# A layer of attention and a gated network on one core: maximum scores and exponent products before gate and up in every slot

## The chip, the core and the metric

One NeuronCore of a Trainium2 chip runs the whole program. The metric is the device time of one execution in microseconds. Five engines take part, each with its own queue that it works off in order: PE (matrix products), ACT (activations, and a DMA queue), DVE (vector), POOL (element-wise work on SBUF), SP (DMA issues). They are held together by semaphores alone.

## What is computed

Sixteen sequences of 256 tokens and width 256 go through one layer with the norm behind each part:

```python
qkv = x @ Wqkv + bqkv                     # 16 query heads of 16, 4 key/value groups
scores = einsum('bqhd,bkhd->bhqk', q, k) / HD
out = softmax(scores) @ v ; x = layernorm(x + out @ Wout + bout)
gate, up = split(x @ ternary(w_gate_up).T)   # 1024 each
h = silu(gate) * up
x = layernorm(x + rms_norm(h) @ ternary(w_proj).T)
```

## The kernel before

The program is a pipeline of slots, eight to a sequence (SLOTS = 8, line 37), 172 in all. Every engine has a function `slot(n)` that lists what it does in slot n, in a fixed order; `run_slots` (line 176) plays slots 0 to 63 written out, 64 to 127 as a loop over 16 slots, and the rest written out. A step starts at an offset (lines 39 to 87) behind the first slot of its sequence: `n.once(X)` is true in one slot of eight, `n.chunk(X)` in eight in a row, one chunk in each. So a slot holds work of up to six sequences at a time. In the middle, a slot with t modulo 8 = m always holds the same work.

What PE does in a slot, in its order (lines 570 to 647):

- gate and up of one chunk of 128 hidden rows (`gate_up`, line 507, chunk offset 31): eight products into ffn_ps. They wait for x1T_lo (the low part of the transposed first norm, once a sequence, slot 7) and for h_done of the chunk before, since ffn_ps has room for one chunk.
- the first maximum group (`max_scores(n, st, 0)`, offset 9): two products into one of three short banks, from which DVE takes the row maxima (line 776).
- the exponent products (`exp_scores`, offset 15): two products of 512 columns into exp_ps, which ACT turns into probs (line 690).
- the steps that come once a sequence: transposes of x (slot 1), v (slot 7), the shift rows (slots 5 and, late, 1), projections of q and k (slot 2), of the output (slot 3), transposes of x1 (slot 5), of pv (slots 6 and 0).
- the second maximum group, probs times v (odd slots), and down (`down`, line 521, offset 33) of a chunk that was gated two slots earlier.

The three short banks are handed out by BANK_TABLE (lines 94 to 101): for each slot modulo 8, which bank each user takes. `use_short` (line 478) makes PE wait until the last user of the same bank has been read. Of it:

```python
BANK_TABLE = {0: {"max0": 1, "pv1": 0, "max1": 2},
...
              2: {"max0": 0, "q": 2, "max1": 0, "k": 1, "att": 2},
              3: {"max0": 0, "max1": 1, "o": 2},
              4: {"max0": 1, "max1": 0},
              5: {"max0": 2, "shift0": 0, "max1": 1, "x1": 2},
              6: {"max0": 0, "pv0": 1, "max1": 0},
              7: {"max0": 2, "v": 0, "max1": 1, "sq": 2}}
```

The user "x1" of slot 5 is released by x1T_lo (line 467), the maximum groups by max_taken.

ACT, in its order (lines 677 to 754): tanh of gate (line 681), the copy of xT (slot 1), the exponent (line 690), q, the copy of pv (slots 3 and 7), the high part of h and its square, the high part of x1T (slot 5), k, the transposed attention, the copy of y (slot 0), and at the end of slots 5 and 1 two DMA issues that put the shift rows of the softmax into q_st (line 746); they wait for DVE's shift_split.

DVE, in its order (lines 811 to 905): the first maximum, gated (line 817), h_f (line 824, releases ffn_ps), the low part of x1T (X1_LOW, slot 6, line 828), the first shift split (slot 5), the residual and statistics of the second norm (LN2_STATS, slot 2, lines 836 to 844), the second maximum, then the division of pv (slots 6, 0), v, the apply step of the first norm (slot 4, line 880), the second shift split (slot 1), the apply step of the second norm (slot 4, line 890), the residual and statistics of the first norm (slot 3, lines 895 to 902), the low part of k.

POOL makes the low part of h and the sum of squares, and SP issues the transfers. SP's stacking of queries and keys for the maximum groups waits for exp_scored (lines 411 and 418).

Of the kernel before, what the change touches and what calls it, by code (L numbers as in the profile page):

```python
# [18 lines left out]
ACT = mybir.ActivationFunctionType  # L19
# [29 lines left out]
EXP0 = 15  # L49
# [9 lines left out]
FFN0 = 31  # L59
# [107 lines left out]
def wait(eng, sem, value):  # L167

    if isinstance(value, int):
        if value > 0:  # L170
            eng.wait_ge(sem, value)
    else:
        eng.wait_ge(sem, value)
# [26 lines left out]
def postln_layer(nc, x, Wqkv, bqkv, Wout, bout, w_gate_up, w_proj, out):  # L200
    ctx = ExitStack()
    with ctx:
        def sb(name, shape, dt=F32):
            return ctx.enter_context(nc.sbuf_tensor(name, shape, dt))

        def ps(name, shape, dt=F32):
            return ctx.enter_context(nc.psum_tensor(name, shape, dt))

        def sem(name):
            return ctx.enter_context(nc.semaphore(name))  # L210
# [46 lines left out]
        probs = sb("probs", [P, 4, TT, 2, S])  # L257
# [29 lines left out]
        exp_ps = ps("exp_ps", [P, TT, 2 * S])  # L287
# [31 lines left out]
        exp_scored, exp_done = sem("exp_scored"), sem("exp_done")  # L319
        pv_done, pv_copied, pv_turned = sem("pv_done"), sem("pv_copied"), sem("pv_turned")  # L320
# [29 lines left out]
        def alternate(n, st):  # L350

            return n.it is None and n.t >= TWO_BANKS and st.s % 2 == 1

        def gate_up_bank(n, st, half):
            return exp_ps[:, half, 0:S] if alternate(n, st) else ffn_ps[:, half, :]
# [86 lines left out]
        def _(pe):  # L442
            def products(dst, lhs, rhs, start=True, stop=True):

                pairs = list(zip(lhs, rhs))
                for i, (a, b) in enumerate(pairs):
                    last = pe.matmul(dst, a, b, start=start and i == 0, stop=stop and i == len(pairs) - 1)  # L447
                return last
# [29 lines left out]
            def use_short(n, name):  # L478

                if found := previous_use(n, SHORT_ORDER.index(name), short_users[BANK[n.t % SLOTS, name]]):  # L480
                    st, (_, _, released, per, extra) = found
                    wait(pe, released, st.count(per, extra))
                return short(n, name)
# [14 lines left out]
            def exp_scores(st):  # L498

                wait(pe, shift_loaded[st.s // 4], st.count(32, 32))  # L500
                wait(pe, exp_done, st.count(8, st.s))
                for t in range(TT):
                    last = pe.matmul(exp_ps[:, t, :], k_st[:, st.par, st.s % 4, t * P:(t + 1) * P],  # L503
                                     q_st[:, st.par, first_head(st.s):first_head(st.s) + 5:4, :], start=True, stop=True)
                last.then_inc(exp_scored, 1)

            def gate_up(n, st):
                wait(pe, x1T_lo, st.count(1, 1))
                if st.it is None and st.b == 0 and st.s == 0:
                    pe.wait_ge(w_ev, len(pieces))  # L510
                if alternate(n, st) and n.t - SLOTS < TWO_BANKS and st.s == 1:
                    wait(pe, exp_done, SLOTS * B)
                wait(pe, h_done, st.count(8, st.s - 1 if n.it is None and n.t > TWO_BANKS else st.s))
                for half in range(2):
                    c = half * F + st.s * P
                    last = products(gate_up_bank(n, st, half),
                                    [wguT[:, k, c:c + P] for k in range(DT) for _ in range(2)],
                                    [x1T[a][:, st.par, k, :] for k in range(DT) for a in range(2)])
                last.then_inc(ffn_made, 1)
# [29 lines left out]
            def turn(bank, src, done):  # L549

                for i, blk in enumerate(src):
                    last = pe.transpose(bank[:, i * P:(i + 1) * P], blk, ident[:])  # L552
                last.then_inc(done, 1)
# [6 lines left out]
            def keep_clock(n, count):  # L560

                if n.it is not None or not CLOCK_FROM <= n.t < CLOCK_TO:
                    return
                turned = sum(at + W_TURN < n.t for at in W_READ)
                if turned:
                    pe.wait_ge(w_ev, turned - 1)
                for _ in range(count):
                    pe.matmul(turn_banks[turned % 2][:, 0, 0:P], ident[:], ident[:], start=True, stop=True)

            def slot(n):  # L570
                if st := n.chunk(FFN0):
                    gate_up(n, st)
                if st := n.chunk(MAX0):
                    if st.it is None and st.b == 0 and st.s == 0:
                        pe.wait_ge(k_ones, 1)
# [3 lines left out]
                if st := n.chunk(EXP0):  # L579
                    exp_scores(st)  # L580
                keep_clock(n, 2)
                if st := n.once(X_T):
                    bank = use_short(n, "x")
                    wait(pe, x_loaded[st.par], st.count2(16, 16))
                    turn(bank, [xn[:, st.par, t, k * P:(k + 1) * P] for k in range(DT) for t in range(TT)], xT_made)
# [55 lines left out]
                if st := n.once(SUM_SQ):  # L641
# [5 lines left out]
                    last.then_inc(sq_summed, 1)  # L647

            run_slots(pe, slot)


        @block.scalar
        def _(act):
# [17 lines left out]
            def high(dst, src):  # L671
                return act.activation(dst, src, ACT.Identity)  # L672

            def both(n, name):
                return short(n, name)[:].rearrange("p (k t) -> p k t", k=2)

            def slot(n):
                if st := n.chunk(FFN0):
                    wait(act, ffn_made, st.count(8, st.s + 1))
                    wait(act, gated_done, st.count(8, st.s - 1))  # L680
                    act.activation(tanh[:, st.s % 2, :], gate_up_bank(n, st, 0), ACT.Tanh, scale=0.5  # L681
                                   ).then_inc(tanh_done, 1)
                if st := n.once(X_HIGH):
                    wait(act, xT_made, st.count(1, 1))
                    wait(act, k_made, st.count(1, 0))
                    high(xT[:], both(n, "x")).then_inc(xT_copied, 1)
                if st := n.chunk(EXP0):
                    wait(act, exp_scored, st.count(8, st.s + 1))
                    wait(act, pv_done, st.count(4, st.s // 2 - 1))
                    act.activation(probs[:, st.s % 4], exp_ps[:], ACT.Exp).then_inc(exp_done, 1)  # L690
                if st := n.once(Q_COPY):
                    if st.it is None and st.b == 0:
                        act.wait_ge(bias_loaded, 16 * 2)
# [59 lines left out]
                if (c := piece(n, 0)) is not None:  # L753
                    read_weights(c)

            run_slots(act, slot)


# [236 lines left out]
```

## Time and profile before

| | |
|---|---|
| median of 3 runs | 626.21 us (624.43 to 627.9) |
| the profiled execution | 624.11 us |
| its span | 622.1 us |
| mean granted TensorE clock | 0.975 |
| PE busy | 556.9 us, 90% |
| DVE busy | 457.7 us, 74% |
| ACT busy | 373.6 us, 60% |
| POOL busy | 288.7 us, 46% |

The span is from the first to the last instruction of the profiled execution; the time of an execution has some 2 us around it. Matmuls overlap in the pipeline, so a row's duration for one matmul is longer than the distance from its start to the next one's start; the distance is what it costs. The arrow behind a row of the timeline names whose end ended the idle time before it.

### The profile page before, as it was taken

What the parts mean: (1) busy time and instruction counts of PE and PEld (TensorE: products, weight loads), DVE (VectorE), ACT (ScalarE), POOL (GpSimd) and SP (SyncE); (2) the same over time, 40 slices, a digit from 0 to 9 for tenths busy, and PEclk for the clock granted to TensorE, in tenths of its full rate; (3) what the DMA queues carried; (4) which work ended last, traced back from release to release, by engine and by line L of the source; (5) the groups of instructions that cost most, each with busy time, mean ns of one, the idle gap of its engine ahead of it and who ended that gap; (6) DMA issues with size and microseconds to landing.
All of it is one profiled execution on the core that took longest, in us unless ns stands there. A gap on an engine that the chain in (4) does not pass through costs nothing.

```text
span 622.1 us, 14146 instructions
## 1 busy us (share of the span) xinstructions
PE 556.9 (90%) x4368; PEld 465.6 (75%) x4368; DVE 457.7 (74%) x1066; ACT 373.6 (60%) x738; POOL 288.7 (46%) x404
## 2 busy tenths in 40 slices
PE   5668989999999999999899999999999999899772
PEld 4656768788788787878787877778787877777762
DVE  7785875777877878787878787877878787755753
ACT  4454645666666666757566666666666756575442
POOL 5432331353536353535435453536354535455763
PEclk9697999999999999999999999999999999999996
DMA  7963354444352517061624344352617070101001
GB/s 232 153 131 44 79 86 95 71 95 69 78 104 69 113 45 138 23 136 25 146 35 115 65 98 80 77 102 61 118 43 136 17 144 5 36 3 35 18 0 35
DMA packets 53932, 49.08 MB, mean 79 GB/s; under 512 B 6144, under 2 KB 53888, under 8 KB 53888
## 3 DMA queue, kind: packets, MB, share of 16 engines
q1 hardware_dynamic: 51152, 47.60, 37.1%
q10 hardware_dynamic: 2736, 0.92, 0.6%
q8 instruction: 24, 0.39, 0.3%
q14 instruction: 20, 0.16, 0.1%
HBM read 33.29 MB, written 14.68 MB: 77 GB/s over the span
## 4 chain that ended last, share of the span: by engine, by line
PE 56%; DVE 25%; issue 9%; POOL 4%; ACT 3%; ACTq 2%; DMA 1%; DVEq 0%; POOLq 0%; SPq 0%
PE ffn_ps L447 13%; PE short_ps L447 10%; PE pv_ps L544 8%; PE short_ps L494 6%; PE exp_ps L503 5%; PE down_ps L529 5%; DVE row_max L776 5%; PE short_ps L552 4%; DVE w_hat L809 3%; DVE gated L817 3%; DVE x L880 2%; DVE st L898 2%; DVE h_f L824 2%; DVE r L895 2%; ACTq L746 2%
## 5 line engine op out<-in xcount | busy, mean ns | idle before, releaser
L776 DVE TENSOR_REDUCE row_max<-short_ps 128x2 f32<-128x512 f32 x256 | 173.7, 682 | 47.5 <-PE short_ps L494 47.4
L933 POOL TENSOR_TENSOR h_lo<-h_f,h_hi 128x256 fp32r<-128x256 f32 x128 | 94.8, 740 | 237.5 <-ACT h_hi L672 227.0
L690 ACT ACTIVATE probs<-exp_ps 128x1024 f32<-128x1024 f32 x128 | 130.9, 1023 | 32.7 <-PE exp_ps L503 30.7
L447 PE MATMUL ffn_ps<-x1T_hi,wguT 128*128 128x256 f32 x480 | 125.6, 295 | 21.0 <-DVE x1T_lo L765 10.7
L494 PE MATMUL short_ps<-k_st,q_st 65*128 65x256 f32 x512 | 116.4, 309 | 12.8 <-DVE row_max L776 12.4
L447 PE MATMUL ffn_ps<-x1T_lo,wguT 128*128 128x256 f32 x480 | 118.8, 281 | 0.0
L447 PEld LDWEIGHTS ffn_ps<-x1T_hi,wguT 128*128 128x128 f32 x480 | 90.4, 188 | 30.5 <-DVE h_f L824 13.9
L681 ACT ACTIVATE tanh<-ffn_ps 128x256 f32<-128x256 f32 x120 | 45.8, 381 | 104.3 <-PE ffn_ps L447 83.3
L494 PEld LDWEIGHTS short_ps<-k_st,q_st 65*128 65x128 f32 x512 | 82.1, 192 | 23.7 <-DVE row_max L776 12.3
L447 PEld LDWEIGHTS ffn_ps<-x1T_lo,wguT 128*128 128x128 f32 x480 | 90.5, 189 | 0.0
L938 POOL TENSOR_TENSOR sq_sum<-sq_sum,h_sq 128x256 f32<-128x256 f32 x112 | 82.9, 741 | 0.0
L503 PE MATMUL exp_ps<-q_st,k_st 67*128 67x512 f32 x256 | 81.2, 398 | 0.1
L529 PE MATMUL down_ps<-wpT,h_hi 128*128 128x256 f32 x256 | 75.7, 318 | 3.4 <-POOL h_lo L933 3.4
L672 ACT ACTIVATE h_hi<-h_f 128x256 fp32r<-128x256 f32 x128 | 52.9, 414 | 35.6 <-DVE h_f L824 33.3
L544 PE MATMUL pv_ps<-probs,v_ones 128*32 128x256 f32 x1024 | 69.4, 389 | 0.0
L529 PE MATMUL down_ps<-wpT,h_lo 128*128 128x256 f32 x256 | 66.4, 281 | 0.0
L817 DVE SCALAR_TENSOR_TENSOR gated<-tanh,ffn_ps 128x256 f32<-128x256 f32 x120 | 49.4, 411 | 17.8 <-ACT tanh L681 17.8
L529 PEld LDWEIGHTS down_ps<-wpT,h_hi 128*128 128x128 f32 x256 | 48.6, 190 | 16.4 <-issue 11.5
L824 DVE TENSOR_TENSOR h_f<-gated,ffn_ps 128x256 f32<-128x256 f32 x120 | 50.5, 421 | 5.4 <-DVE gated L817 1.6
L529 PEld LDWEIGHTS down_ps<-wpT,h_lo 128*128 128x128 f32 x256 | 48.7, 190 | 0.4
L447 PE MATMUL short_ps<-xT,wqkv 128*128 128x256 f32 x192 | 47.5, 384 | 0.0
L722 ACT ACTIVATE h_sq<-h_f 128x256 f32<-128x256 f32 x112 | 45.2, 404 | 0.0
(98 smaller groups left out, 864.6 us busy)
## 6 DMA issues: line engine op xcount, KB each, us to landing
q_st<-q_dram SPq DMA_DIRECT2D x128, 128.0 KB, 4.1
q_dram<-q_p SPq DMA_DIRECT2D x16, 512.0 KB, 3.0
xn<-in_L_attn_x_dram SPq DMA_DIRECT2D x16, 256.0 KB, 4.6
k_st<-k_dram SPq DMA_DIRECT2D x64, 64.0 KB, 2.3
res<-in_L_attn_x_dram SPq DMA_DIRECT2D x16, 256.0 KB, 3.3
out_dram<-y_out SPq DMA_DIRECT2D x16, 256.0 KB, 2.2
wgu_raw<-in_L_ffn_w_gate_up_dram SPq DMA_DIRECT2D x8, 256.0 KB, 6.5
k_dram<-k_p SPq DMA_DIRECT2D x16, 128.0 KB, 3.1
```

The costliest lines, as they stand in the source:

```text
L447: last = pe.matmul(dst, a, b, start=start and i == 0, stop=stop and i == len(pairs) - 1)
L494: last = pe.matmul(bank[:, t * S:(t + 1) * S], q_st[0:PAD, st.par, head, t * P:(t + 1) * P], k_st[0:PAD, st.par, st.s % 4, :], start=True, ...
L503: last = pe.matmul(exp_ps[:, t, :], k_st[:, st.par, st.s % 4, t * P:(t + 1) * P], q_st[:, st.par, first_head(st.s):first_head(st.s) + 5:4, ...
L529: last = pe.matmul(down_ps[:, t, :], h_p[a][:, st.s % 4, t * P:(t + 1) * P], wpT[:, st.s, :], start=(st.s == 0 and t == 0 and a == 0), sto ...
L544: last = pe.matmul(pv_ps[r:r + 32, s % 4 // 2, :], v_ones[:, st.par, t, s % 4, :], probs[:, s % 4, t, i, :], start=(t == 0), stop=(t == TT ...
L672: return act.activation(dst, src, ACT.Identity)
L690: act.activation(probs[:, st.s % 4], exp_ps[:], ACT.Exp).then_inc(exp_done, 1)
L776: dve.tensor_reduce(row_max[:, st.par, head * TT:(head + 1) * TT], short(n, f"max{i}")[:].rearrange("p (t k) -> p t k", t=TT), AX.X, ALU.m ...
L817: dve.scalar_tensor_tensor(gated[:, st.s % 2, :], tanh[:, st.s % 2, :], 1.0, gate_up_bank(n, st, 1), ALU.add, ALU.mult).then_inc(gated_don ...
L824: dve.tensor_tensor(h_f[:, st.s % 2, :], gated[:, st.s % 2, :], gate_up_bank(n, st, 0), ALU.mult).then_inc(h_done, 1)
L933: pool.tensor_tensor(h_p[1][:, st.s % 4, :], h_f[:, st.s % 2, :], h_p[0][:, st.s % 4, :].bitcast(F32), ALU.subtract).then_inc(h_lo, 1)
L938: pool.tensor_tensor(sq_sum[:, st.par, :], sq_sum[:, st.par, :], h_sq[:, st.s % 2, :], ALU.add).then_inc(h_summed, 1)
```

## The change

In PE's `slot`, the call of `gate_up` moves from the front of the slot to behind the first maximum group and the exponent products (and behind the clock-keeping products of `keep_clock`, which exist only in slots 2 to 29). In ACT's `slot`, the exponent moves in front of tanh, and so also in front of the copy of xT. DVE, POOL and SP keep their order; BANK_TABLE, SHORT_ORDER and every semaphore count stay as they are. The diff in full:

```diff
--- before.py
+++ after.py
@@ -568,8 +568,6 @@
                     pe.matmul(turn_banks[turned % 2][:, 0, 0:P], ident[:], ident[:], start=True, stop=True)
 
             def slot(n):
-                if st := n.chunk(FFN0):
-                    gate_up(n, st)
                 if st := n.chunk(MAX0):
                     if st.it is None and st.b == 0 and st.s == 0:
                         pe.wait_ge(k_ones, 1)
@@ -579,6 +577,8 @@
                 if st := n.chunk(EXP0):
                     exp_scores(st)
                 keep_clock(n, 2)
+                if st := n.chunk(FFN0):
+                    gate_up(n, st)
                 if st := n.once(X_T):
                     bank = use_short(n, "x")
                     wait(pe, x_loaded[st.par], st.count2(16, 16))
@@ -675,6 +675,10 @@
                 return short(n, name)[:].rearrange("p (k t) -> p k t", k=2)
 
             def slot(n):
+                if st := n.chunk(EXP0):
+                    wait(act, exp_scored, st.count(8, st.s + 1))
+                    wait(act, pv_done, st.count(4, st.s // 2 - 1))
+                    act.activation(probs[:, st.s % 4], exp_ps[:], ACT.Exp).then_inc(exp_done, 1)
                 if st := n.chunk(FFN0):
                     wait(act, ffn_made, st.count(8, st.s + 1))
                     wait(act, gated_done, st.count(8, st.s - 1))
@@ -684,10 +688,6 @@
                     wait(act, xT_made, st.count(1, 1))
                     wait(act, k_made, st.count(1, 0))
                     high(xT[:], both(n, "x")).then_inc(xT_copied, 1)
-                if st := n.chunk(EXP0):
-                    wait(act, exp_scored, st.count(8, st.s + 1))
-                    wait(act, pv_done, st.count(4, st.s // 2 - 1))
-                    act.activation(probs[:, st.s % 4], exp_ps[:], ACT.Exp).then_inc(exp_done, 1)
                 if st := n.once(Q_COPY):
                     if st.it is None and st.b == 0:
                         act.wait_ge(bias_loaded, 16 * 2)
```

## Rows read from the trace of the kernel before

**Rows 1.** The page's first part: busy us, share of the span, instructions.

```profile
PE 556.9 (90%) x4368; PEld 465.6 (75%) x4368; DVE 457.7 (74%) x1066; ACT 373.6 (60%) x738; POOL 288.7 (46%) x404
```

**Rows 2.** Windows: PE, PEld, DVE, ACT, POOL busy (instructions), PEclk, DMA share, GB/s.

```profile
342.59:375.82 33.23, 32.08 (x256) 26.77 (x257) 25.84 (x63) 21.58 (x44) 15.99 (x24) 1.00 0.41 84
560.00:590.00 30.00, 25.48 (x205) 22.38 (x204) 20.54 (x52) 14.89 (x37) 18.66 (x28) 1.00 0.07 18
```

**Rows 3.** Waits of PE, 75 to 575 us: total us, times, longest.

```profile
PE ffn_ps L447 <- DVE h_f L824: 9.0, 16, 1.0
PE ffn_ps L447 <- DVE x1T_lo L765: 8.4, 14, 1.3
PE short_ps L494 <- DVE row_max L776: 4.3, 4, 1.5
```

**Rows 4.** Timeline of PE, slots 3 to 5: start us, duration us, line, tiles.

```profile
337.99 0.66 PE L552 MATMUL short_ps<-ident,x 128*128 128x128 f32 x4
...
359.49 0.28 PE L447 MATMUL ffn_ps<-x1T_hi,wguT 128*128 128x256 f32 x1
...
360.44 0.40 PE L494 MATMUL short_ps<-k_st,q_st 65*128 65x256 f32 x2
360.68 0.63 PE L503 MATMUL exp_ps<-q_st,k_st 67*128 67x512 f32 x2
361.15 0.40 PE L494 MATMUL short_ps<-k_st,q_st 65*128 65x256 f32 x2
...
364.78 0.28 PE L447 MATMUL ffn_ps<-x1T_hi,wguT 128*128 128x256 f32 x1
...
367.81 0.39 PE L447 MATMUL ffn_ps<-x1T_hi,wguT 128*128 128x256 f32 x1 [0.50 <-DVE h_f L824]
```

**Rows 5.** Timelines of PE and of ACT, slot 4: exponent products, then the exponent.

```profile
365.97 0.62 PE L503 MATMUL exp_ps<-q_st,k_st 67*128 67x512 f32 x2
...
366.63 1.03 ACT L690 ACTIVATE probs<-exp_ps 128x1024 f32<-128x1024 f32 x1 [0.32 <-PE exp_ps L503]
```

**Rows 6.** Timeline of ACT, slot 6 (ACTq: its queue, issuing a DMA).

```profile
339.79 0.61 ACTq L746 DMA_DIRECT2D q_st<-shift_lo  x1
340.56 0.38 ACT L681 ACTIVATE tanh<-ffn_ps 128x256 f32<-128x256 f32 x1 [0.61 <-PE ffn_ps L447]
340.84 1.02 ACT L690 ACTIVATE probs<-exp_ps 128x1024 f32<-128x1024 f32 x1
341.89 0.42 ACT L672 ACTIVATE h_hi<-h_f 128x256 fp32r<-128x256 f32 x1
```

**Rows 7.** Timeline of PE: first rows of slot 6 and of slot 7.

```profile
338.97 0.28 PE L447 MATMUL ffn_ps<-x1T_hi,wguT 128*128 128x256 f32 x1
...
342.59 0.39 PE L447 MATMUL ffn_ps<-x1T_hi,wguT 128*128 128x256 f32 x1 [0.51 <-DVE x1T_lo L765]
```

**Rows 8.** Timeline of ACT, slot 2.

```profile
355.42 0.61 ACTq L746 DMA_DIRECT2D q_st<-shift_lo  x1
356.20 0.38 ACT L681 ACTIVATE tanh<-ffn_ps 128x256 f32<-128x256 f32 x1 [1.84 <-issue]
```

**Rows 9.** Timeline of DVE, slot 6.

```profile
340.98 0.42 DVE L817 SCALAR_TENSOR_TENSOR gated<-tanh,ffn_ps 128x256 f32<-128x256 f32 x1
...
341.77 0.68 DVE L765 TENSOR_TENSOR x1T_lo<-short_ps,x1T_hi 128x512 fp32r<-128x512 f32 x1
```

**Rows 10.** Timeline of DVE, slots 5, 2 (three rows) and 4.

```profile
337.26 0.67 DVE L776 TENSOR_REDUCE row_max<-short_ps 128x2 f32<-128x512 f32 x1
...
356.62 0.42 DVE L817 SCALAR_TENSOR_TENSOR gated<-tanh,ffn_ps 128x256 f32<-128x256 f32 x1 [0.48 <-ACT tanh L681]
...
357.41 0.87 DVE L836 SCALAR_TENSOR_TENSOR r<-y_sb,inv,x 128x256 f32<-128x256 f32 x2
...
359.27 0.67 DVE L776 TENSOR_REDUCE row_max<-short_ps 128x2 f32<-128x512 f32 x1
...
366.89 0.41 DVE L817 SCALAR_TENSOR_TENSOR gated<-tanh,ffn_ps 128x256 f32<-128x256 f32 x1
```

## The prediction

> **What bounds the kernel now.** The page's first part comes first: PE is busy for 90% of the span [rows 1]. Then the windows: one turn of the pipeline (eight slots, from slot 7 to the next slot 7) lasts 33.23 us and holds 32.08 us of PE work, at a granted clock of 1.00, which is 2.4 GHz [rows 2]. So in the middle PE is the bound and 1.15 us a turn is all that another order can win. Third, the waits of PE in that stretch: 16 times for h_f, 14 times for x1T_lo, four times for row_max [rows 3], so the first two are one a turn. The reader is to see in them where the 1.15 us lie: 0.50 us in front of gate and up of slot 5 (h_f) [rows 4], 0.51 us in front of those of slot 7 (x1T_lo) [rows 7], and 0.14 us in smaller pieces. PE hardly ever waits for a bank (row_max). Last, the timelines of the three engines: which instruction of ACT and DVE is late where, and how much room is left.
>
> I name slots by t modulo 8, and S is a slot's start on PE. A group of gate and up takes PE 0.95 us (359.49 to 360.44), a first maximum group M 0.24 us (to 360.68), the exponent products E 0.47 us (to 361.15) [rows 4]. Old order: gate/up at S, M at S+0.95, E at S+1.19. New order: M at S, E at S+0.24, gate/up at S+0.71. Either way the three end at S+1.66. No instruction, byte or wait is added; waits come earlier or later in their queues, and that is all that can cost.
>
> **Part A: the exponent in front of tanh, on ACT.** In a slot where ACT is free this costs nothing: exp_ps is ready 0.66 us after E starts (365.97 to 366.63 [rows 5]), so at S+0.90; an exponent holds ACT for 1.05 us (340.84 to 341.89 [rows 6]), so tanh can start at S+1.95, and gate/up, which started at S+0.71, are only ready at about S+1.9. But two slots of eight begin with ACT late. The two DMA issues of the shift rows (line 746) stand at the end of ACT's slots 5 and 1, behind a wait for DVE. The second issue ends at 340.40 in slot 6 (339.79 plus 0.61), the slot having begun at 338.97 [rows 6, 7], and tanh follows at 340.56, the exponent behind it [rows 6] (its row names PE as the releaser, but gate/up had been issued by 338.97 + 0.95 = 339.92; the issue came last). With the order turned round the exponent (ready at S+0.90 = 339.87) takes the place at 340.56 and tanh comes at 341.61: 1.05 us later. The same in slot 2: second issue until 356.03, tanh at 356.20 [rows 8], after the change at 357.25.
>
> *Slots 6 and 7.* gated follows tanh by 0.42 us, and x1T_lo starts 0.79 us after gated [rows 6, 9]. PE stands still for x1T_lo already: 0.51 us of idle, then gate/up of slot 7 at 342.59 [rows 7]. All of 1.05 us therefore reaches PE. One would hope that M and E, now in front, fill the gap. They can't: M of slot 7 uses bank 2 (BANK_TABLE), whose user before it is x1 of slot 5, and its release is x1T_lo itself. So the whole slot starts when gate/up would have: **+1.05 us a turn**, 13 times (t = 38 to 134; at t = 142 no shift DMA is left): **+13.7 us**. Bounds: 0 if ACT had room, and 1.05 plus the 0.71 us of M and E if these lay in series with anything, which the code doesn't show; I take the value of the rows.
>
> *Slots 2 and 3.* tanh, gated and h_f slip by 1.05 us. h_f itself isn't urgent in this long slot, but DVE does the statistics of the second norm next, and only then the maximum of the second group: gated at 356.62, r at 357.41, row_max at 359.27 [rows 10]. A wait of PE on a bank ends 0.73 us after such a row_max starts (337.26 [rows 10] to 337.99 [rows 4], the turn of x1). Today bank 0 is thus free at 360.00, 0.51 us after slot 3 begins at 359.49 [rows 4]; nobody notices, since M comes at 360.44, covered by gate/up. After the change M of slot 3 stands at the queue's head and wants this very bank 0 (second group of slot 2 and M of slot 3 share it). Its cover is gone: 0.51 us plus 1.05 us = **1.56 us of new idle a turn**, with E and gate/up queued behind M. It happens where the second norm runs in slot 2 and a maximum follows in slot 3, t = 42 to 130, 12 times: **+18.7 us**. Bounds: 0.51 us (the order on PE alone, 6 us in all) and 1.56 us plus the longest wait of this kind on record, 1.5 us [rows 3].
>
> **Part B: gate and up later, on PE.** Slot 5 gains: its gate/up need h_f of slot 4 and now have M and E in front. But what counts in slots 4 and 5 is DVE's queue, from the first norm's residual in slot 3 through both norms' apply steps to the maximum of M in slot 5; the turn of x1 waits for that maximum (bank 2 again: row_max at 337.26 [rows 10], PE at 337.99 [rows 4]). So the 0.50 us are only moved. Does this DVE chain get longer? In slot 4 gated starts at 366.89 [rows 10]. With S = 364.78 [rows 4], exp_ps is ready at 365.68, tanh starts at 366.73 and gated at 367.15: **0.26 us later**, 12 times: **+3.1 us**. Between 0 and 0.5 us a turn are possible.
>
> The 0.14 us of small idle (slots 0 and 1, gate/up waiting for h_f) go, since h_f has 0.71 us more: **-0.12 us** 13 times, **-1.6 us**.
>
> **Costed at nothing.** exp_scored comes 0.95 us earlier, and SP's stacking of queries and keys waits for it (lines 411 and 418): those transfers serve a slot some six later, DMA is busy 0.41 of the turn [rows 2], and without that cover a late one would cost its delay once a turn. Y_COPY now stands in front of an exponent in slot 1 and may push its tanh by 0.6 us; slot 1's second maximum then frees bank 0 some 0.3 us late for slot 2, but the wait of slot 2 for the shift DMA absorbs it. Slots before t = 31 have no gate/up, slots from 143 no exponent: nothing changes there.
>
> **Sum.** 13.7 + 18.7 + 3.1 - 1.6 = +33.9 us. The profiled execution took 624.1 us (span 622.1), so 658.0 us. It lies 2.1 us below the median of the runs shown, 626.21; for a median I add these: **660 us**. A turn should grow from 33.23 to about 35.9 us.
>
> **Rivals.**
> *R1, faster.* The mechanism is the cover of M and E in front of gate/up: if ACT has room in slots 2 and 6 (if the DMA issue doesn't hold the exponent as it holds tanh), h_f and x1T_lo are asked for 0.71 us later and all the idle of a turn, 1.15 us, goes: 13 x 1.15 = 15 us, 611 us. For it speaks that PE's two large waits [rows 3] both stand in front of gate/up. Against it: line 746 on ACT's own queue [rows 6, 8], and the banks. It decides at a delay of tanh under 0.2 us in slot 6 and a row_max of slot 2 over 0.5 us earlier than I have it. 5%.
> *R2, one wait of the two.* Slot 3 doesn't stall in full (DVE catches up): 660 - 18.7 = 641 us; or slot 7 doesn't: 646 us. For it speaks that a queue shifted as a whole may find new room; against it that both paths are without a gap in the rows. 14%.
> *R3, nothing.* The turned order leaves the same last waits and they end when they did, because the DVE chain of slots 3 to 5 sets the turn and the rest has slack: 626 us. Against it: PE's idle is 1.15 us a turn, so slack is scarce. 4%.
> *R4, the clock falls.* The granted clock of the turn shown is 1.00 [rows 2]; in the drain, with PE busy 25.48 of 30 us (15% idle), it is 1.00 too [rows 2], and after the change PE would be idle about 3.9 of 35.9 us, 11%. If it fell to 1.2 GHz nonetheless behind the two new waits, slot 3 (5.29 us, 359.49 to 364.78 [rows 4]) and slot 7 (taken as a mean slot, 33.23 / 8 = 4.15 us) would double: 12 x 9.4 = 113 us, 773 us. The Trainium skill, TensorE: Matmul & The Clock Gate, section A second HAM failure mode: psum-queue depth-cycling, speaks for it: a kernel that cycles through PSUM banks idles a little between its matmul groups so often that the clock swings between its two levels. By that rule this kernel should swing already; the rows at 1.00 don't show it. 3%.
>
> **How the numbers follow.** Forecast 74%, R1 5%, R2 14%, R3 4%, R4 3%. The forecast's own spread comes from its bounds: each of the two waits 0.3 us more or less a turn is 8 us, some late turn of DVE or a second issue of long duration a few more: 650 to 671. To leave no more than 2 in 10 out, the range takes in R2 nearly whole: **642 to 671**. About 0.5% (3 us) is what a measurement of this kernel can tell from no change. Faster by more: R1, 0.05. Within: R3, 0.04. Slower: 0.91.
>
> **What would show it.** Right: PE's waits list row_max in front of M (line 494) some 12 times with 1.5 us and x1T_lo now in front of M, not of gate/up, with about 1.6 us; in slot 6 the exponent directly behind the DMA issue and tanh 1.05 us later; h_f gone as a reason for PE's waits but for slot 5; clock 1.00; PE busy unchanged at 557 us, share down to 85%. Wrong: tanh of slots 2 and 6 no later than now, or M of slot 3 without idle before it; a row_max of slot 2 that waits for PE rather than for DVE's statistics; a turn under 34 us.

## The result and the profile after

The changed kernel takes 660.36 us (median of 4 runs, 657.91 to 663.27) against 625.32 us (median of 4, 623.56 to 627.9): 1.056 times as long, 95% interval 1.050 to 1.062. The forecast was 660 us, range 642 to 671. Ratios and intervals leave out the runs that are more than 1.5% above the fastest of their kernel (below: two of e2's four, one each of e4's, of e7's and of the last group's kernel before); medians are over all runs. The profiled execution has a span of 659.4 us at a mean granted clock of 0.964 (before: 622.1 us, 0.975).

First part of the page, then PE's waits between 141 and 545 us (total us, times, longest), of the changed kernel:

```profile
PE 568.9 (86%) x4368; PEld 472.7 (72%) x4368; DVE 460.5 (70%) x1066; ACT 365.7 (55%) x738; POOL 288.6 (44%) x404
...
PE short_ps L494 <- DVE x1T_lo L765: 12.9, 12, 1.1
PE short_ps L494 <- DVE row_max L776: 11.4, 15, 0.9
PE short_ps L552 <- DVE row_max L776: 9.1, 11, 0.9
```

[rows 3] named gate and up (L447) as what waited, for h_f and for x1T_lo. In this stretch nobody waits there any more. What waits are the two maximum groups at the head of slots 7 and 3 (L494) and the turn of x1 in slot 5 (L552), about once a turn each; row_max comes a few times more, for M of slot 2. The waits are shorter than forecast (1.5 us for row_max and 1.6 for x1T_lo): 0.9 and 1.1 us at most; where the rest went is worked out in the section on why the prediction was right.

Windows of the changed kernel: a turn in the middle, the first turn with gate and up, and two pieces of the last full one (PE, PEld, DVE, ACT, POOL busy, then PEclk, DMA share, GB/s).

```profile
359.79:395.30 35.51, 32.46 (x256) 26.88 (x256) 26.06 (x64) 21.00 (x43) 15.97 (x23) 1.00 0.37 78
...
110.91:146.36 35.45, 33.30 (x249) 27.19 (x247) 23.70 (x54) 20.79 (x41) 13.08 (x18) 0.95 0.42 79
...
547.00:556.00 9.00, 5.98 (x52) 4.61 (x50) 6.19 (x18) 4.95 (x11) 5.29 (x8) 1.00 0.02 5
556.00:565.00 9.00, 8.27 (x41) 6.19 (x42) 2.85 (x8) 2.62 (x5) 2.56 (x5) 0.62 0.00 1
```

The turn has gone from 33.23 us [rows 2] to 35.51 us, with 32.46 us of PE busy for 32.08 (the same matmuls, a few rows longer behind a wait): 1.9 us more of every turn are idle. The last two rows are something the prediction did not have: PE is busy for only 5.98 of 9 us, and in the 9 us behind it is granted 0.62 of its clock.

The starts of PE's slots in a turn, changed kernel (slots 7, 1, 2, 3 and 4, the turn of x1 in slot 5, then slots 6 and 7):

```profile
360.52 0.50 PE L494 MATMUL short_ps<-k_st,q_st 65*128 65x256 f32 x2 [1.10 <-DVE x1T_lo L765]
...
367.65 0.40 PE L494 MATMUL short_ps<-k_st,q_st 65*128 65x256 f32 x2
...
371.99 0.51 PE L494 MATMUL short_ps<-k_st,q_st 65*128 65x256 f32 x2
...
378.60 0.50 PE L494 MATMUL short_ps<-k_st,q_st 65*128 65x256 f32 x2 [0.90 <-DVE row_max L776]
...
383.99 0.40 PE L494 MATMUL short_ps<-k_st,q_st 65*128 65x256 f32 x2
...
390.59 0.66 PE L552 MATMUL short_ps<-ident,x 128*128 128x128 f32 x4 [0.85 <-DVE row_max L776]
...
391.88 0.50 PE L494 MATMUL short_ps<-k_st,q_st 65*128 65x256 f32 x2
...
396.03 0.50 PE L494 MATMUL short_ps<-k_st,q_st 65*128 65x256 f32 x2 [1.09 <-DVE x1T_lo L765]
```

From these and the same starts of the kernel before:

| slots | before, us | after, us | difference | forecast |
|---|---|---|---|---|
| 7, 0 | 7.25 | 7.13 | -0.12 | -0.12 |
| 1, 2 | 9.65 | 10.95 | +1.30 | +1.56 |
| 3 | 5.29 | 5.39 | +0.10 | 0 |
| 4, 5, 6 | 11.04 | 12.04 | +1.00 | +0.26 + 1.05 |
| turn | 33.23 | 35.51 | +2.28 | +2.75 |

The chain behind slot 3's wait, in the turn before it (turns of the two parities differ a little, here 35.87 us and 35.51): ACT, then DVE, then PE.

```profile
337.61 0.61 ACTq L746 DMA_DIRECT2D q_st<-shift_lo  x1
338.39 1.02 ACT L681 ACTIVATE probs<-exp_ps 128x1024 f32<-128x1024 f32 x1 [1.63 <-PE exp_ps L503]
339.31 0.38 ACT L685 ACTIVATE tanh<-ffn_ps 128x256 f32<-128x256 f32 x1
...
339.72 0.42 DVE L817 SCALAR_TENSOR_TENSOR gated<-tanh,ffn_ps 128x256 f32<-128x256 f32 x1 [1.91 <-ACT tanh L685]
...
340.51 0.87 DVE L836 SCALAR_TENSOR_TENSOR r<-y_sb,inv,x 128x256 f32<-128x256 f32 x2
...
342.37 0.66 DVE L776 TENSOR_REDUCE row_max<-short_ps 128x2 f32<-128x512 f32 x1
...
343.09 0.50 PE L494 MATMUL short_ps<-k_st,q_st 65*128 65x256 f32 x2 [0.80 <-DVE row_max L776]
```

Read downwards: the second DMA issue ends at 338.22; the exponent takes the place that tanh had in [rows 8]; tanh, gated, the norm's residual r, and only then the row_max that frees bank 0; M of slot 3 starts 0.72 us later. It is the chain of the prediction, link by link. One number in it differs: from the exponent's start to tanh's it is 0.92 us, not 1.05.

### The profile page after: what moved, and what is told of

The parts are those of the page before. It is cut to its first block, busy times and chain, and to the rows that moved or that the text cites. A ratio compares the mean times of both kernels' runs of the same rounds, so it can differ in the third digit from the quotient of the medians.

```text
span 659.4 us, 14146 instructions
## 1 busy us (share of the span) xinstructions
PE 568.9 (86%) x4368; PEld 472.7 (72%) x4368; DVE 460.5 (70%) x1066; ACT 365.7 (55%) x738; POOL 288.6 (44%) x404
## 4 chain that ended last, share of the span: by engine, by line
PE 39%; DVE 29%; issue 13%; ACT 8%; ACTq 4%; POOL 4%; DMA 1%; DVEq 0%; POOLq 0%; SPq 0%
PE ffn_ps L447 9%; DVE row_max L776 6%; PE short_ps L494 6%; PE short_ps L447 6%; PE pv_ps L544 6%; PE exp_ps L503 5%; DVE gated L817 5%; ACT tanh L685 4%; ACTq L746 4%; DVE x L880 3%; DVE w_hat L809 3%; PE down_ps L529 3%; DVE h_f L824 2%; PE short_ps L552 2%; DVE y_out L890 2%
## 5 line engine op out<-in xcount | busy, mean ns | idle before, releaser
L494 PE MATMUL short_ps<-k_st,q_st 65*128 65x256 f32 x512 | 122.9, 322 | 43.1 <-DVE row_max L776 26.4
L447 PE MATMUL ffn_ps<-x1T_hi,wguT 128*128 128x256 f32 x480 | 123.0, 289 | 5.3 <-DVE x1T_lo L765 3.5
L494 PEld LDWEIGHTS short_ps<-k_st,q_st 65*128 65x128 f32 x512 | 80.2, 193 | 59.9 <-DVE row_max L776 32.5
L447 PE MATMUL ffn_ps<-x1T_lo,wguT 128*128 128x256 f32 x480 | 120.5, 284 | 0.0
L447 PEld LDWEIGHTS ffn_ps<-x1T_hi,wguT 128*128 128x128 f32 x480 | 91.9, 191 | 17.8 <-issue 5.9
L447 PEld LDWEIGHTS ffn_ps<-x1T_lo,wguT 128*128 128x128 f32 x480 | 92.3, 192 | 4.0
L447 PE MATMUL short_ps<-xT,wqkv 128*128 128x256 f32 x192 | 47.5, 383 | 0.0
```

The source lines that it names most:

```text
L494: last = pe.matmul(bank[:, t * S:(t + 1) * S], q_st[0:PAD, st.par, head, t * P:(t + 1) * P], k_st[0:PAD, st.par, st.s % 4, :], start=True, ...
```

## The experiments

Twelve kernels were run, in three groups, each against fresh runs of the kernel before (medians 625.1 to 625.9 us). "Turn" is the mean distance of x1T_lo over the eleven turns in the middle: 33.32 us before, 35.61 us changed.

| run | us | ratio, 95% interval | turn, us |
|---|---|---|---|
| changed kernel | 660.4 | 1.056 (1.050 to 1.062) | 35.61 |
| e1 PE's half | 646.3 | 1.036 (1.031 to 1.041) | 34.77 |
| e2 ACT's half | 728.9 | 1.155 (1.145 to 1.166) | 40.03 |
| e3 maximum before norm | 646.3 | 1.037 (1.032 to 1.042) | 34.50 |
| e4 tanh first in 2 and 6 | 645.4 | 1.031 (1.025 to 1.036) | 34.59 |
| e5 changed, issues on SP | 640.1 | 1.026 (1.021 to 1.032) | 34.55 |
| e6 before, issues on SP | 623.0 | 0.994 (0.991 to 0.997) | 33.24 |
| e7 PE's half, DVE moves | 623.3 | 0.996 (0.994 to 0.999) | 33.21 |
| e8 before, DVE moves | 619.0 | 0.990 (0.987 to 0.994) | 33.17 |
| e9 changed, DVE moves | 626.6 | 1.003 (1.000 to 1.006) | 33.51 |
| e10 e8 with issues on SP | 614.9 | 0.984 (0.981 to 0.986) | 33.05 |
| e11 gate/up first in slot 3 | 649.7 | 1.038 (1.034 to 1.042) | 34.82 |
| e12 wait filled | 656.8 | 1.054 (1.049 to 1.058) | 35.67 |

### The two halves

**e1**, PE's order new, ACT's old. Against the changed kernel:

```diff
-                (exponent); (tanh); (copy of xT)
+                (tanh); (copy of xT); (exponent)
```

> PE's half of the change alone: M and E in front of gate and up, ACT with tanh in front of the exponent as before. My theory (the cost sits in ACT's order where ACT is late, and in two maximum groups that lose their cover): slot 3 keeps only the lost cover, 0.5 us a turn; slot 7 loses 0.5 us since gate and up of slot 6 are ready 0.7 us later than before; a turn of about 34.3 us, 639 us in all. A rival, that the cost comes from gate and up standing later on PE whatever ACT does, expects nearly all of the change here: 655 to 660 us. A third, that the two halves only work together and PE's alone stalls because the exponent frees exp_ps late, expects over 660 us.

646.3 us: 21 of the 35 us come from PE's half alone, where 14 were expected. Its waits, 145 to 525 us:

```profile
PE short_ps L494 <- DVE x1T_lo L765: 9.2, 11, 0.8
PE exp_ps L503 <- ACT probs L690: 5.0, 11, 0.5
PE short_ps L494 <- DVE row_max L776: 4.1, 11, 0.6
```

x1T_lo costs 0.84 us a turn here and 1.1 in the changed kernel; row_max in front of M costs 0.4 against 1.0 (there 11.4 us in these eleven turns): my mechanism. The second row is what I had left out: with tanh in front, ACT frees exp_ps late, and the exponent products, now early in the slot, wait for it (0.45 us a turn). The third rival was right about the mechanism, wrong about the size.

**e2**, ACT's order new, PE's old.

```diff
                 (ACT's slot, kernel before)
-                (tanh); (copy of xT); (exponent)
+                (exponent); (tanh); (copy of xT)
```

> ACT's half alone: the exponent in front of tanh, PE as before (gate and up first). The exponent products come 1.2 us into the slot, so tanh can't start before 2.9 us and the next gate and up not before 4.24 us after a slot's start: the short slots 0, 4 and 6 grow by 1.2 to 1.3 us each, slot 3 waits 0.6 us: a turn of some 37.5 us, 681 us in all. The rival that puts the cost on PE's order expects 630 us or less here.

728.9 us, 48 more than expected, and its runs lie far apart (716 to 739 us); the two that the ratio rests on took 716.2 and 726.4 us. The profiled one took 731.3 us, but a low clock is in all four: 0.896 to 0.929 over the span, against 0.967 to 0.976 in the kernel before. Windows of three turns, then PE's waits in the first and in the second of them:

```profile
474.25:511.77 37.52, 32.53 (x256) 26.87 (x256) 25.87 (x63) 21.27 (x43) 16.03 (x23) 1.00 0.37 74
431.90:474.25 42.35, 37.16 (x256) 30.22 (x256) 25.97 (x63) 21.35 (x43) 15.96 (x23) 0.88 0.32 66
552.71:590.27 37.56, 32.57 (x256) 26.88 (x256) 25.86 (x64) 21.30 (x43) 16.02 (x23) 1.00 0.36 74
...
PE ffn_ps L447 <- DVE h_f L824: 2.7, 2, 1.6
PE ffn_ps L447 <- DVE x1T_lo L765: 1.7, 1, 1.7
...
PE ffn_ps L447 <- DVE h_f L824: 3.0, 2, 1.6
PE ffn_ps L447 <- DVE x1T_lo L765: 1.7, 1, 1.7
```

Two turns run at a granted clock of 1.00 and last 37.52 and 37.56 us: the 37.5 us expected. The other eleven between 110 and 633 us have 0.88 to 0.96, last 38.8 to 42.4 us, and hold up to 37.2 us of PE work instead of 32.5. The fourteenth turn is at 0.75 and takes 40.7 us, where the kernel before needs 28.0. The waits in front of gate and up are nearly the same in both windows, three a turn, 4.4 and 4.7 us together, the longest 1.7 us. So where the clock falls behind such waits, idle PE time costs twice; but what decides whether it falls these rows don't show, since nearly the same waits stand in turns at 1.00. The Trainium skill, TensorE: Matmul & The Clock Gate, section A second HAM failure mode: psum-queue depth-cycling, says that many short idle stretches between matmul groups can make the clock swing between its levels. In e2 it does, in most turns and not in all (1.7 us the longest wait, 5.0 us idle in a turn at full clock); in the middle of the changed kernel it does not (1.1 us, 3.05 us a turn).

The halves do not add: PE's costs 21 us, ACT's 104 us (96 by the two shorter runs), both together 35. The exponent in front of tanh only makes sense where the exponent products are early, and PE's new order takes away most of what ACT's costs.

### Which slots, and which waits

**e4**, tanh in front again in slots 2 and 6 alone.

```diff
+                late = n.t % SLOTS in (2, 6)
-                if st := n.chunk(EXP0):
+                if (st := n.chunk(EXP0)) and not late:
...
+                if (st := n.chunk(EXP0)) and late:      # behind tanh
```

> The changed kernel, but ACT takes tanh in front of the exponent in slots 2 and 6 alone, the two that begin behind DMA issues; the other six keep the new order. My theory: slot 2 gives back 1.06 us, slot 6 0.5 us (gate and up are ready only 2.15 us into it): 12.5 x 1.57 = 19.6 us less, 641 us, the same as with the old order in all eight. The rival, that the new order costs a little in every slot, expects 655 us.

645.4 us, a turn 1.02 us shorter (1.57 were expected). Two slots of eight carry all of the cost of ACT's order: leaving the new order in the other six is no worse than the old one in all (e1, 34.77).

**e5** and **e6**, the DMA issues on SP's queue.

```diff
                 (ACT's slot)
-                for half in range(2):
-                    if st := n.once(SHIFT_T[half]):
-                        wait(act, shift_split, ...); act.dma_start(...) x2
                 (SP's slot, in front of STORE)
+                        sp_wait(shift_split, ...); sp.dma_start(...) x2
```

> The changed kernel, the four DMA issues a turn of the shift rows moved from ACT's queue to SP's (same transfers, same waits). ACT is then free at the start of slots 2 and 6. My theory: tanh 1.35 us earlier in slot 2 and 0.4 us earlier in slot 6: 12.5 x 1.76 = 22 us less, 638 us. If the issues on ACT don't matter: 660 us. If SP's queue holds the shift rows up, PE's exponent products wait for them by name and it is slower.

> The kernel before with the same move of the issues to SP. My theory: in the old order ACT's lateness is hidden (in slot 6 DVE is with the first maximum until the same moment at which tanh ends, slot 2 has 2 us of room): 625 us, within 3 us. If the issues cost in themselves: 610 to 618 us.

In the changed kernel this brings 20 us (a turn 1.06 us shorter, where 1.76 were expected; another 7 us are the first turn and the thirteenth, which now keep a clock of 1.00), in the kernel before 2 to 3 us (0.08 us a turn). The same issues cost seven times as much under the new order: what makes ACT late is hidden until the exponent is put in front of tanh.

**e3**, on DVE the second maximum in front of the second norm's statistics.

```diff
+                if st := n.chunk(MAX0):
+                    take_maximum(n, st, 1)
                 if st := n.once(LN2_STATS):
...
-                if st := n.chunk(MAX0):
-                    take_maximum(n, st, 1)
```

> The changed kernel, with one more move: in DVE's slot 2 the maximum of the second group stands in front of the second norm's residual and statistics (1.86 us of DVE work). If M of slot 3 stalls because bank 0 is freed behind these, its wait goes wholly: 12 x 1.57 = 19 us less, 641 us. If the stall is set by something else in slot 2 (ACT's k or attention copy, DVE's whole load), it stays: over 655 us.

646.3 us; a turn 1.11 us shorter, not 1.57. The waits of maximum groups for row_max between 145 and 525 us fall from 15 to four (the turn of x1 waits for it as before, 9.2 us in eleven turns):

```profile
PE short_ps L494 <- DVE x1T_lo L765: 11.7, 11, 1.1
...
PE short_ps L494 <- DVE row_max L776: 2.0, 4, 0.5
```

So slot 3's wait came from DVE's order and is gone; but it had been 1.0 to 1.1 us long and not 1.57, and a rest of 0.2 us a turn stays (2.0 us in eleven turns). The rest stands in front of M of slot 2, 0.5 us in every other turn, and waits for slot 1's second maximum, behind Y_COPY and the exponent. The prediction had seen that one and put it down as absorbed; it is absorbed only as long as slot 3 waits behind it.

**e11**, gate and up in front in slot 3 alone.

```diff
+                if (st := n.chunk(FFN0)) and n.t % SLOTS == 3:
+                    gate_up(n, st)
...
-                if st := n.chunk(FFN0):
+                if (st := n.chunk(FFN0)) and n.t % SLOTS != 3:
```

> The changed kernel, PE with gate and up in front again in slot 3 of the eight alone. They cover 0.95 us of the wait for bank 0 that the trace of the changed kernel shows there (about 1.4 us against the kernel before): 12 x 0.95 = 11 us less, 649 us. If the whole slot is late for another reason, it stays at 660 us.

649.7 us, as expected. The cover that gate and up gave slot 3 is worth 11 us.

**e9**, the changed kernel with all three moves on DVE (e3's, x1T_lo in front of slot 6's first maximum, and the second norm's apply step one slot later):

```diff
+                if st := n.once(X1_LOW):
+                    ...
                 if st := n.chunk(MAX0):
                     take_maximum(n, st, 0)
...
-LN2_APPLY = 44
-STORE = 44
+LN2_APPLY = 45
+STORE = 45
```

> The changed kernel, both halves, with the three moves on DVE. If the loss comes from the two maximum groups that wait behind late DVE work and from nothing else, it goes nearly whole: x1T_lo no longer stands behind the late gated, the second maximum of slot 2 no longer behind the norm; a turn of 33.2 us, 622 us. If ACT's order has a cost of its own in every slot: over 632 us.

626.6 us, a turn of 33.51 us: of the 2.29 us that the change costs a turn, 2.10 are gone. That flatters it, for the moves help the kernel before as well (e8, below: 619.0 us, a turn of 33.17). Against e8 the change still costs 7.6 us, 0.35 us a turn. So about four fifths of the 35 us were these waits for late DVE work; waits for row_max remain (8.1 us in the middle, e8 5.3), and the rest is not worked out.

### The clock in the last full turn

**e12** fills the longest wait of the changed kernel behind its start-up, which stands in slot 131:

```diff
+                if n.it is None and n.t == 131:
+                    fill(n.chunk(EXP0))    # this slot's exponent products, 6 times more
                 if st := n.chunk(MAX0):
```

M of slots 130 and 131 in the changed kernel, with the exponent products behind it:

```profile
550.28 0.50 PE L494 MATMUL short_ps<-k_st,q_st 65*128 65x256 f32 x2 [0.38 <-DVE row_max L776]
...
556.73 0.62 PE L494 MATMUL short_ps<-k_st,q_st 65*128 65x256 f32 x2 [3.38 <-DVE row_max L776]
557.15 1.05 PE L503 MATMUL exp_ps<-q_st,k_st 67*128 67x512 f32 x2
```

The same two rows of e12, and its window for the 9 us behind:

```profile
549.16 0.50 PE L494 MATMUL short_ps<-k_st,q_st 65*128 65x256 f32 x2 [0.37 <-DVE row_max L786]
...
555.61 0.50 PE L494 MATMUL short_ps<-k_st,q_st 65*128 65x256 f32 x2 [0.48 <-DVE row_max L786]
...
556.00:565.00 9.00, 8.95 (x69) 7.44 (x69) 6.11 (x14) 4.69 (x10) 2.79 (x6) 1.00 0.00 1
```

> The changed kernel, with the exponent products of slot 131 issued six times more, in front of its first maximum group, where PE waits 3.4 us for row_max in the changed kernel and is granted 0.62 of its clock in the 9 us behind. The extra products (2.8 us) lie inside the wait. If the lower clock is what makes that turn 38.4 us: granted clock 1.00 there, the turn some 4 us shorter, 656 us. If the turn is long from the wait alone: 660 us, or more where the filling runs over.

M of slot 131 starts 6.45 us after M of slot 130 in both (550.28 to 556.73, 549.16 to 555.61): the filling neither shortens the wait for row_max nor runs over it, it only leaves 0.48 us of it idle instead of 3.38. Behind it the granted clock is 1.00 instead of 0.62, and the turn is 35.29 us instead of 38.37. So 3.1 us of that turn are the clock's. The totals, 656.8 us against 660.4, go the same way, but their runs overlap (655.1 to 661.1 and 657.9 to 663.3): it is the trace that shows it.

### A faster version

> A version that may beat both: PE in the new order, ACT in the old one, and three moves on DVE: x1T_lo in front of the first maximum in slot 6, the second maximum in front of the second norm's statistics in slot 2, the second norm's apply step one slot later. With DVE no longer behind, M and E can do what they might: cover the waits in front of gate and up. By slots: 6 shorter by 0.4 us than before, 4 and 5 by 0.3, 0 by 0.1: a turn of 32.4 us, 615 us. If PE's new order is a cost in itself it stays above 626 us.

> The kernel before with the three moves on DVE alone. By slots: slot 7's wait for x1T_lo becomes one for h_f of 0.26 us, slot 5's wait of 0.5 us stays, the turn of x1 comes 0.13 us earlier: 0.55 us a turn, 618 us. Against the run with PE's new order this tells what that order is worth once DVE isn't behind.

> The kernel before with the three moves on DVE and the four DMA issues on SP. The issues on SP alone gave 0.6%, the moves alone 1%; if they don't overlap: 615 us, if the same waits are paid once: 618 to 619 us.

e7 (PE's new order, ACT's old, DVE moves) takes 623.3 us, e8 (the order before, DVE moves) 619.0, e10 (e8 with the issues on SP) 614.9 us, 0.984 times the kernel before (0.981 to 0.986). The turns of e7 and e8, 33.21 and 33.17 us, miss the 32.4 and 32.7 us that I had expected. Between 145 and 525 us the wait for x1T_lo (6.0 us in the kernel before) is gone in both, but 5.3 us (e8) and 6.5 us (e7) for row_max come in its place; e8 keeps the 5.7 us for h_f, and e7 waits 5.0 us for probs instead. What e8 gains lies mostly outside the middle: its first turn is 30.69 us against 32.42, its thirteenth 31.00 against 33.31. Once DVE is no longer behind, PE's new order still brings nothing over the old one: it costs 4.3 us (e7 against e8).

## Why the prediction was right

**Right in mechanism.** Both waits stand where they were put, held by the banks that were named, at the head of slots 7 and 3, and h_f is gone from PE's waits in the middle. e3, e4, e5 and e11 each take out one link (DVE's order, ACT's order in slots 2 and 6, the DMA issue, the lost cover), and each gives back 11 to 20 us; e9, which takes DVE's lateness away in both places, leaves 1.5 us of the 35 against the kernel before, and 7.6 us against e8, the kernel before with the same moves. The rivals: R1 asked for ACT to be free, which only e5 gives, and even then the kernel is slower than before. R2 and R3 are out: both waits are there, though each is shorter than the prediction's signs said.

**Mis-sized.** The step "an exponent holds ACT for 1.05 us (340.84 to 341.89 [rows 6])" misread a row. What starts at 341.89 is h_hi, and h_hi needs h_f. DVE's timeline of the kernel before:

```profile
341.43 0.42 DVE L824 TENSOR_TENSOR h_f<-gated,ffn_ps 128x256 f32<-128x256 f32 x1
```

h_f ends at 341.85, and h_hi starts 0.04 us later: it had waited for DVE, not for the exponent. Where nothing else is late, the next activation starts 0.92 us behind the exponent's start (338.39 to 339.31 above). The Trainium skill, ScalarE: Activation LUTs, section What ACT_TABLE_LOAD costs, would have warned me: for 1024 elements it gives 0.186 us + 1024 x 0.833 ns = 1.04 us, less an overlap of 0.093 us with the next activation, an estimate of 0.95 us; the trace, at 0.92 us, nearly agrees. The length enters three terms, and with 0.92 us slots 4 to 6 come to 0.13 + 0.92 = 1.05 (measured 1.00), slots 1 and 2 to 0.51 + 0.92 = 1.43 (measured 1.30 and, in the turn of the other parity, 1.67). A turn then grows by 2.36 us; measured over eleven turns, 2.29 us, and forecast 2.75.

**In the right group, not all in the right place.** The groups of slots agree better than their parts. The same points in the kernel before:

```profile
353.97 0.37 PE L447 MATMUL ffn_ps<-x1T_hi,wguT 128*128 128x256 f32 x1
...
371.22 0.66 PE L552 MATMUL short_ps<-ident,x 128*128 128x128 f32 x4
```

And DVE's shift split of slot 5 in the changed kernel:

```profile
391.54 0.28 DVE L787 SCALAR_TENSOR_TENSOR shift_lo<-short_ps,shift_hi 16x128 fp32r<-16x128 f32 x1
```

From slot 2's start to slot 3's it is 6.61 us instead of 5.52 (353.97 to 359.49): +1.09, not 1.56. The other 0.21 of the 1.30 stand in front of M of slot 2 (0.67 in the turn of the other parity), which the prediction had costed at nothing. With PE's half alone (e1) slot 2 takes 6.01 us: +0.49, the 0.51 us of lost cover. From slot 4's start to the turn of x1 it is 0.16 us more (6.44 to 6.60; 0.13 by the corrected length), from there to slot 7's start 0.84 us more (4.60 to 5.44; 0.92). But 0.31 of these 0.84 fall in front of M of slot 6, which now stands at the head of its slot and needs bank 0, read last by the shift split of slot 5. The split ends at 391.82 and M starts at 391.88 (from x1's turn to slot 6 it is 1.29 us instead of 0.98); the prediction has no such wait. Slot 7's own is shorter by as much, since its end hangs on the DMA issue behind that split and not on slot 6's start.

**Missed, and of the other sign.** Eleven turns at 2.29 us are 25.2 us, not the 30 of the forecast, which left under 4 us for everything else. The total came out all the same because the ends cost 12 us. Between the two profiled executions, whose spans differ by 37.3 us, that is the first turn 3.0 us (35.45 against 32.42), the thirteenth 5.1 us (38.37 against 33.31), the rest 4 us, of which 1.6 lie ahead of the first turn. There the programs differ in one thing alone, the exponent in front of the copy of xT in slots 17 and 25, and the stretch varies from run to run (e6, which has the old order too, is 1.7 us shorter there than the kernel before). It is not the wait alone that makes the thirteenth turn long. In slot 130 there are no projections of q and k any more, so the slot is short, and M of slot 131 waits 3.38 us for row_max instead of 0.9; but it waited in the kernel before too, even behind gate and up:

```profile
526.04 0.50 PE L494 MATMUL short_ps<-k_st,q_st 65*128 65x256 f32 x2 [1.17 <-DVE row_max L776]
```

With the wait filled (e12) this turn is 35.29 us, 1.98 more than before: no worse than a turn in the middle. What my sum lacks there is the clock, 3.1 us. In the first turn it falls too; the exponent products of slot 31, and the window around them, then the same window of e7 and of e9:

```profile
113.24 1.22 PE L503 MATMUL exp_ps<-q_st,k_st 67*128 67x512 f32 x2 [1.09 <-DMA q_st<-shift_lo]
...
112.00:116.00 4.00, 2.91 (x13) 2.57 (x12) 1.53 (x5) 1.63 (x2) 0.00 (x0) 0.65 0.76 147
...
112.00:116.00 4.00, 3.25 (x31) 2.38 (x32) 3.11 (x10) 1.87 (x4) 0.00 (x0) 1.00 0.91 154
...
112.00:116.00 4.00, 4.00 (x29) 2.93 (x27) 2.28 (x6) 1.41 (x2) 0.00 (x0) 0.57 1.05 158
```

The exponent products wait 1.09 us for the shift rows' DMA, and the clock is 0.65. Gate and up stood in front of them before; the prediction looked at the turns in the middle and costed nothing at that end. R4, the falling clock, was right about two stretches and wrong about the middle: I gave it all or nothing. The trace of the kernel before had such a place too, in its start-up, which the prediction did not look at: M waits 3.15 us for row_max, and in the 4 us behind the wait the clock is 0.50:

```profile
47.74 0.80 PE L494 MATMUL short_ps<-k_st,q_st 65*128 65x256 f32 x2 [3.15 <-DVE row_max L776]
...
48.00:52.00 4.00, 4.00 (x19) 3.75 (x20) 1.38 (x2) 0.76 (x1) 1.46 (x2) 0.50 0.89 117
```

So 660 us is right by its mechanism and by half of its terms; to within 1 us it is right by chance.

Not tried: how far the first turn's 3.0 us are the DMA's and how far the clock's. e5, whose issues stand on SP, has that turn at 32.65 us and a clock of 1.00, which speaks for the issues on ACT as the beginning of it. But e7 has its issues on ACT and stays at 1.00 too (32.24 us), with waits of 0.86 us for row_max and 0.46 for the DMA in front; e9, with 0.86 and 0.36, falls to 0.57. So the issues alone don't decide it, and what does stays open.

## What to carry to other kernels

Before work is moved away from the head of an in-order slot, ask what wait it covers for the work that moves up; here the moved-up group shares its bank with work that DVE reads late, and 0.51 us of hidden lag came out as 0.49 us more in slot 2 with PE's half alone, and as 1.0 to 1.1 us once ACT was late as well. A reordering of one engine should be costed in the slots in which that engine starts late, not in the typical one: two slots of eight carried ACT's whole cost. And the fill and the drain have slots of other lengths, where the same wait can be three times as long and take the clock with it. A fix has to be judged against the old kernel with the same fix: against the plain one, e9 had lost 1.5 us, against e8 7.6.

## What the runs showed of the hardware

In the changed kernel a single idle stretch of 3.4 us on PE was followed by 9 us at a mean granted clock of 0.62, between the levels of 1.2 and 2.4 GHz; filling the stretch with products of no use brought 3 us of that turn. In e2, with waits of at most 1.7 us, three a turn, the clock was lower in eleven of thirteen turns and stayed at 1.00 in two, with nearly the same waits. The turns at 1.00 differ by 0.04 us (37.52 and 37.56); those below differ from each other by 3.5 us. In the middle of the changed kernel, with waits of at most 1.1 us and 3.05 us idle in a turn, it stayed at 1.00. In the first turn, e7 and e9 have nearly the same two waits on PE (0.86 and 0.46 us, 0.86 and 0.36), and in the window from 112 to 116 us one is granted 1.00 and the other 0.57.
